# Folding the expert weights on TensorE, first rows in 13 pieces, and spare matrix products in an audio-tower kernel

## The reference, cut to what matters

```python
h = tok(x)                          # per feature: softplus/log gates and a log-space scan over 257 rows
h = h + attn(layernorm(h))          # 8 heads, 16 wide; sequence b attends to sequence b +- 4
h = h + ffn(layernorm(h))           # 16 experts, top 2, and one shared expert, all swiglu5
def ffn(x):
    h  = x @ w1 + b1                            # 128 -> 2*96 per expert
    g  = clip(h[..., ::2], -c0, c0); u = clip(h[..., 1::2], -c1, c1)
    t  = g * sigmoid(g * alpha) * scale * (u + shift)
    y += weight[expert] * (t @ w2 + b2)
```

## Time and profile before

| | |
|---|---|
| median of 3 runs | 325.62 us (325.33 to 325.69) |
| the profiled execution's own time | 325.96 us |
| its span, first to last instruction | 324.1 us |
| mean granted TensorE clock | 0.896 |
| busy: PE, DVE, ACT, POOL | 275.7, 255.6, 186.6, 128.8 us |

### The profile page before, as it was taken

The page is one execution under the profiler, slowest core; times in us unless marked ns, Lnnn a source line. Parts: engine busy times, 40 slices in busy tenths (PEclk is TensorE's granted clock), DMA queues, the critical chain, the costliest instruction groups (busy, mean ns, idle before and its releaser), DMA issues.

```text
span 324.1 us, 5121 instructions
## 1 busy us (share of the span) xinstructions
PE 275.7 (85%) x1764; PEld 169.3 (52%) x1764; DVE 255.6 (79%) x421; ACT 186.6 (58%) x297; POOL 128.8 (40%) x92
## 2 busy tenths in 40 slices
PE   3903941738998899999999999999999999999994
PEld 1301321305553666664466665566676699856641
DVE  1096878797559998779978879799578997599972
ACT  2757398653786878746487885186394620441151
POOL 2031959580204245582004437030735900654700
PEclk9965895575899999999999999999999975899798
DMA  6920000000000000000000000010010000000002
GB/s 235 418 91 0 0 2 0 2 0 0 2 2 1 1 2 3 0 2 0 0 3 2 0 1 2 2 33 2 0 34 0 2 0 0 3 1 0 2 1 65
DMA packets 3515, 7.41 MB, mean 23 GB/s; under 512 B 281, under 2 KB 2465, under 8 KB 3234
## 3 DMA queue, kind: packets, MB, share of 16 engines
q1 hardware_dynamic: 3490, 7.08, 5.9%
HBM read 6.03 MB, written 1.05 MB: 22 GB/s over the span
## 4 chain that ended last, share of the span: by engine, by line
PE 75%; issue 9%; DVE 9%; ACT 3%; DMA 1%; POOL 1%; DVEq 0%; SPq 0%; ACTq 0%
PE bank L1152 73%; DVE mxt L911 2%; PE bank L1155 2%; DVE w1l L805 2%; DMA cst<-in_consts 1%; DVE yr L976 1%; POOL z L461 1%; DVE tr L1008 1%; POOL z L466 1%; DVE vr L986 0%; ACT l L593 0%; DVE tr L1028 0%; DVE lt L832 0%; ACT osb L732 0%; DVE w L1046 0%
## 5 line engine op out<-in xcount | busy, mean ns | idle before, releaser
L527 POOL TENSOR_TENSOR vr<-vr,cwb 128x1024 f32<-128x1024 f32 x24 | 58.7, 2453 | 14.8 <-DVE vr L986 10.2
L1152 PE MATMUL bank<-tr,w 128*128 128x512 f32 (+1 forms) x104 | 50.0, 616 | 0.0
L911 DVE TENSOR_REDUCE mxt<-bank 128x2 f32<-128x512 f32 x64 | 40.5, 684 | 11.4 <-PE bank L1152 11.4
L1152 PE MATMUL bank<-xh,w1h 128*128 128x512 f32 x104 | 47.2, 454 | 0.8 <-DVE vr L986 0.8
L675 ACT ACTIVATE pt<-bank 128x512 f32<-128x512 f32 x64 | 33.8, 604 | 24.1 <-PE bank L1152 24.1
L726 ACT ACTIVATE tr<-yr,fpar 128x1024 f32<-128x1024 f32 (+1 forms) x28 | 30.0, 1086 | 27.0 <-PE bank L1152 17.0
L976 DVE TENSOR_SCALAR yr<-bank,fpar 128x512 f32<-128x512 f32 x52 | 40.2, 804 | 5.9 <-PE bank L1152 5.7
L521 POOL TENSOR_SCALAR vr<-vr,fpar 128x1024 f32<-128x1024 f32 x12 | 16.0, 1334 | 68.4 <-ACT vr L714 68.4
L1152 PE MATMUL bank<-xh,w1l 128*128 128x512 f32 x104 | 41.6, 400 | 0.0
L1152 PE MATMUL bank<-xl,w1h 128*128 128x512 f32 x104 | 41.4, 398 | 0.0
L1008 DVE SCALAR_TENSOR_TENSOR tr<-tr,yr 128x1024 f32<-128x1024 f32 (+1 forms) x28 | 33.5, 1213 | 2.8 <-ACT tr L726 2.7
(11 more groups left out here) (182 smaller groups left out, 480.8 us busy)
## 6 DMA issues: line engine op xcount, KB each, us to landing
pt<-in_w1a SPq DMA_DIRECT2D x1, 1672.0 KB, 9.3
tr<-in_w1b SPq DMA_DIRECT2D x1, 1672.0 KB, 12.4
xt<-in_x SPq DMA_DIRECT2D x4, 256.0 KB, 9.2
out<-osb SPq DMA_DIRECT2D x8, 128.0 KB, 1.9
w<-in_w SPq DMA_DIRECT2D x1, 832.0 KB, 14.1
cst<-in_consts SPq DMA_DIRECT2D x1, 488.5 KB, 5.0
cst<-in_consts SPq DMA_DIRECT2D x1, 193.5 KB, 4.3
vr<-in_shift SPq DMA_DIRECT2D x1, 6.5 KB
```

The lines of the kernel that those rows point to most:

```text
L527: g.tensor_tensor(vr[:, n % NV, :, :], vr[:, n % NV, :, :], cwb[:, u % 2, :].unsqueeze(1).to_broadcast([P, 2, W]), ALU.mult).then_inc(S["v ...
L911: last = v.tensor_reduce(top_of, ps.bank("mx", u, s, c, t)[:, :].rearrange("p (i t) -> p i t", i=2), AX_X, ALU.max)
L1152: return nc.tensor.matmul(out_, lhsT, rhs, start=start, stop=stop, **k)
```

## The change

- **Weights folded by TensorE.** `w1_row` is now 2 rows (the true row 0, and the shifts), where it was 128 (1672.0 KB). The transfer of `shift`, the pieces `w1s`, `w1p` and `gw` go. A new piece `wp` makes 7 parts of 512 columns (the last 256 and the 16 gate columns): identity by `w1_raw`, plus a 2-row product with a new constant `bsel`, both fp32, into one bank. `w1h` and `w1l` read the bank instead of `w1_raw`, and `w1l` releases it. A `g` or `u` product waits only for the parts that hold its columns; the first `pt` and `th` of unit 0 wait until the parts have been folded.
- **First rows in 13 pieces.** `zg` is 13 pieces of 4 products: the high weights by the high and low activations side by side (16 columns), and the low weights by the high ones (8 columns). `zclip` gets two more VectorE operations and clips out of SBUF. All pieces of the first rows move ahead of unit 3's experts, most of them into unit 2's attention.
- **Spare products.** 28 pieces `spare`, each of two fp32 products with 256 columns whose result nobody reads. Each waits for a milestone, a count of a semaphore of units 0 and 1 (`SPARE`), and takes and frees a bank.
- **All tables are new**: order on every engine and banks.

The new order of TensorE's pieces, up to the experts of unit 0: z.0.2 z.0.0 z.0.1 z.1.0 lsum.0 lsum.1 z.1.2 z.1.1 spare0 wp0 z.2.2 z.2.1 spare2 spare1 spare3 z.2.0 spare5 center.0.1 wp1 wp3 var.0.1 wp2 spare8 k.0 lsum.2 wp4 z.3.1 spare24 q.0 spare21 v.0 wp5 spare22 wp6 spare7 spare9 mx.0.0.0 mx.0.0.1 spare23 z.3.2 spare25 z.3.0 center.1.1 spare26 spare6 mx.0.1.0 nmt.0.0 spare10 var.1.1 spare4 lsum.3 mx.0.1.1 spare12 o0.0.0 spare27 st.0.0.0 nmt.0.1 q.1 k.1 st.0.0.1 pv.0.0.0 st.0.1.0 pv.0.0.1 st.0.1.1 o0.0.1 v.1 spare16 pv.0.1.0 mx.1.0.0 pv.0.1.1 mx.1.0.1 spare13 mx.1.1.0 center.0.2 spare17 center.2.1 mx.1.1.1 var.2.1 var.0.2 nmt.1.0 spare18 spare14 st.1.0.0 st.1.0.1 gate.0. Behind that, spare20 and spare19 stand in unit 0's experts, and spare15 and spare11 between the last `down` pieces of unit 3. The new `zg` order: zg.0 zgate zg.1 to zg.5, st.2.1.0, zg.6 to zg.9, st.2.1.1, down.1.4, zg.10 to zg.12, zcw, o0.2.1, pv.2.1.0, pv.2.1.1, mx.3.0.0, zd.

VectorE's new order: t.0 d.0 hg.0 l.0 w.0 mscan.0 dw.0 lf.0 w1l.0 sscan.0 w2s h1.0 w1l.1 xn.0.1 l.1 w1l.2 w.1 xsum.0 mscan.1 w1l.3 dw.1 l.2 w1l.4 w1l.5 w1l.6, and then the maxima of unit 0 with sscan.1, w.2, mscan.2, dw.2 and sscan.2 between them.

```diff
+SPARE = (("l3", 1), ("ll", 1), ("m", 2), ("dw", 1), ("s", 2), ("ef", 1), ("h1", 1), ("sq1", 1), ("rs1", 1), ("xs", 1), ("mz", 1),
+         ("mz", 2), ("nm", 2), ("nm", 4), ("lden", 1), ("lden", 2), ("h2", 1), ("h2", 2), ("sq2", 1), ("rs2", 1), ("xh", 1),
+         ("l3", 2), ("ll", 2), ("m", 4), ("dw", 2), ("s", 4), ("h1", 2), ("rs1", 2))
...
-            def w1p(u, k):
-                pool.wait_ge(s_w1s, 1)
-                pool.wait_ge(s_w1b, 16)
-                g.tensor_tensor(w1_raw[:, w1_part(k)], w1_raw[:, w1_part(k)], w1_row[:, w1_part(k)], ALU.subtract).then_inc(s_w1p, 1)
...
             def w1l_(u, k):
                 dve.wait_ge(s_w1h, k + 1)
-                v.tensor_tensor(w1l[:, w1_part(k)], w1_raw[:, w1_part(k)], w1h[:, w1_part(k)].bitcast(F32), ALU.subtract)\
-                    .then_inc(s_w1l, 1)
+                last = v.tensor_tensor(w1l[:, w1_part(k)], ps.bank("wp", 0, k)[:, 0:n], w1h[:, w1_part(k)].bitcast(F32), ALU.subtract)
+                ps.release(last, "wp", 0, k)
...
+            def wp(u, k):
+                pe.wait_ge(s_const, 16)
+                pe.wait_ge(s_w1a, 16)
+                pe.wait_ge(s_w1b, 16)
+                ps.take(pe, "wp", 0, k)
+                cols = slice(k * W, min((k + 1) * W, W1COLS + E))
+                o = ps.bank("wp", 0, k)[:, 0:cols.stop - cols.start]
+                mm(o, ident, w1_raw[:, cols], stop=False)
+                ps.fill(mm(o, const("bsel")[0:2, :], w1_row[:, cols], start=False), "wp", 0, k)
+
+            def spare(u, i):
+                ge(pe, *SPARE[i])
+                ps.take(pe, "spare", 0, i)
+                o = ps.bank("spare", 0, i)
+                ps.fill(mm(o[:, 0:T], wtok[:, 0:P], xt[:, 0, 0:T]), "spare", 0, i)
+                ps.release(mm(o[:, T:W], wtok[:, 0:P], xt[:, 0, T:W]), "spare", 0, i)
...
-                        mm(o, w1h[:, cols], zxh[:, :], stop=False)
-                        mm(o, w1h[:, cols], zxl[:, :], start=False, stop=False)
-                        last = mm(o, w1l[:, cols], zxh[:, :], start=False)
...
+                    mm(o, w1h[:, cols], zxs[:, :, :].rearrange("p k b -> p (k b)"), stop=False, skip_group_check=True)
+                    last = mm(o[:, 0:B], w1l[:, cols], zxs[:, 0, :], start=False, skip_group_check=True)
```

More of the change, by code:

```diff
@@ L34 @@
 for _name, _n in (("wtok", 3 * P), ("btok", 3), ("omat", P), ("cmat", P), ("wq", P), ("wk", P), ("wv", P), ("ident", P),
-                  ("head", 2), ("row", 2), ("nrow", 2), ("ones32", 64), ("e0sel", P), ("b2s", 1), ("par", 10)):
+                  ("head", 2), ("row", 2), ("nrow", 2), ("ones32", 64), ("e0sel", P), ("bsel", P), ("b2s", 1), ("par", 10)):
     CONSTS[_name] = (_at, _at + _n)
@@ L79, in unit_pieces @@
     f += [("yo", u), ("out", u), ("store", u)]
+    if u == 0:
+        a += [("spare", 0, i) for i in range(len(SPARE))]
     z = []
     if u == UNITS - 1:
-        z += [(n, 0) for n in ("zv", "zc", "zvar", "zrs", "zxn", "zone", "zsplit", "zgate", "zr1", "zexp", "zr2", "zcw", "zg",
-                               "zclip", "zth", "zgg", "zte", "zd", "zy", "zout", "zstore")]
+        z += [(n, 0) for n in ("zv", "zc", "zvar", "zrs", "zxn", "zone", "zsplit", "zgate", "zr1", "zexp", "zr2", "zcw")]
+        z += [("zg", 0, c) for c in range(NC)]
+        z += [(n, 0) for n in ("zclip", "zth", "zgg", "zte", "zd", "zy", "zout", "zstore")]
     return t + a + f + z
-SETUP_PIECES = [("w1s", 0)] + [(n, 0, k) for k in range(W1_PARTS) for n in ("w1p", "w1h", "w1l")] + [("gw", 0), ("w2s", 0)]
+SETUP_PIECES = [(n, 0, k) for k in range(W1_PARTS) for n in ("wp", "w1h", "w1l")] + [("w2s", 0)]
 PIECES = SETUP_PIECES + [p for u in range(UNITS) for p in unit_pieces(u)]
@@ L201, in filled_by @@
         return [("y0", u)]
-    one_bank = ("z", "lsum", "center", "var", "q", "k", "v", "nmt", "o0", "gate", "cwb", "g", "u", "out",
-                "zv", "zc", "zvar", "zgate", "zcw", "zg", "zd", "zout")
+    if name == "zg":
+        return [("zg", 0)] if numbers[0] == 0 else []
+    one_bank = ("wp", "spare", "z", "lsum", "center", "var", "q", "k", "v", "nmt", "o0", "gate", "cwb", "g", "u", "out",
+                "zv", "zc", "zvar", "zgate", "zcw", "zd", "zout")
     return [piece] if name in one_bank else []
@@ L339, in build @@
         s_zout = sem("first_rows_stored")
-        s_soft, s_w2s, s_w1s = sem("clamps"), sem("w2_scaled"), sem("w1_shifted")
-        s_w1p, s_w1h, s_w1l, s_gw = sem("w1_rows_taken"), sem("w1_high"), sem("w1_low"), sem("gate_weights")
+        s_soft, s_w2s = sem("clamps"), sem("w2_scaled")
+        s_w1h, s_gw = sem("w1_high"), sem("gate_weights")
         names = ("rh e3 l3 lp t d hg rl el ll w m dw ed s lf ef h1 sq1 sq2 rs1 rs2 xs one xh xl mz nm pv lden rd h2 "
-                 "rt rexp cwr gcv gcg ucv ucg th gg vcg vcv teg tev down zsq zrs zone zsplit zrt zexp zcwr zth zgg zte").split()
+                 "rt rexp cwr gcv gcg ucv ucg th gg vcg vcv teg tev down zsq zrs zone zsplit zg zsum zclip zrt zexp zcwr zth zgg zte").split()
         S = {n: sem("r_" + n) for n in names}
@@ L549, in zone @@
                 g.memset(zt[0:1, 4, :], 1.0).then_inc(S["zone"], 1)
-            run("G", {"w1p": w1p, "t": t_, "d": d_, "hg": hg, "dw": dw, "lf": lf, "h1": h1_, "h2": h2, "one": one_, "xl": xl_,
+            run("G", {"t": t_, "d": d_, "hg": hg, "dw": dw, "lf": lf, "h1": h1_, "h2": h2, "one": one_, "xl": xl_,
                       "gc": gate_clip, "uc": up_clip, "vc": weigh, "te": te, "zone": zone})
@@ L671, in pt_ @@
                 if u == 0 and s == 0:
-                    act.wait_ge(s_w1l, W1_PARTS)
-                    act.wait_ge(s_gw, 1)
+                    for k in range(W1_PARTS):
+                        ps.filled(act, "wp", 0, k)
                 ge(act, "pv", n - NPT + 1)
@@ L721, in th @@
                 if u == 0:
-                    act.wait_ge(s_gw, 1)
+                    for j in range(W1_PARTS):
+                        ps.filled(act, "wp", 0, j)
                 clipped(act, "g", GATE_BY, n, "gcv", "gcg")
@@ L767, in zth @@
                 act.wait_ge(s_par, PARS)
-                ps.released(act, "zg", 0)
+                ge(act, "zclip", 4)
                 for r, of in enumerate((slice(0, ROUTED), slice(ROUTED, NC))):
@@ L1090, in zclip @@
                 dve.wait_ge(s_par, PARS)
-                z = ps.bank("zg", 0)[:, 0:2 * NC * B].rearrange("p (k c b) -> p k c b", k=2, b=B)
+                z = ps.bank("zg", 0)[:, 0:4 * NC * B].rearrange("p (k c r b) -> p k c r b", k=2, c=NC, b=B)
+                v.tensor_copy(zsp, z[:, :, :, 1, :]).then_inc(S["zsum"], 1)
+                ge(dve, "zsum", 1)
+                last = v.tensor_tensor(zy[:, 0:2, :, :], z[:, :, :, 0, :], zsp, ALU.add)
+                ps.release(last, "zg", 0)
+                ps.released(dve, "zg", 0)
                 for kind, hi, lo in ((0, GHI, GLO), (1, UHI, ULO)):
                     for r, of in enumerate((slice(0, ROUTED), slice(ROUTED, NC))):
-                        last = v.tensor_scalar(zy[:, kind, of, :], z[:, kind, of, :], fpar[:, hi, r:r + 1], fpar[:, lo, r:r + 1],
-                                               ALU.min, ALU.max)
-                ps.release(last, "zg", 0)
+                        v.tensor_scalar(zy[:, kind, of, :], zy[:, kind, of, :], fpar[:, hi, r:r + 1], fpar[:, lo, r:r + 1],
+                                        ALU.min, ALU.max).then_inc(S["zclip"], 1)
             def zgg(u):
@@ L1141, in _ @@
             dve.wait_ge(s_bias, BIASES)
-            run("V", {"w1s": w1s, "w1l": w1l_, "gw": gw, "t": t_, "d": d_, "hg": hg, "l": l_, "w": w_, "mscan": mscan, "dw": dw,
+            run("V", {"w1l": w1l_, "t": t_, "d": d_, "hg": hg, "l": l_, "w": w_, "mscan": mscan, "dw": dw,
                       "sscan": sscan, "lf": lf, "h1": h1_, "h2": h2, "xn": xn, "xsum": xsum, "mr": mr, "mz": mz,
@@ L1271, in half_ @@
                 ge(pe, "xl", u + 1)
-                pe.wait_ge(s_w1l, W1_PARTS)
+                for k in sorted({(2 * c + kind) * P // W, ((2 * c + kind + 1) * P - 1) // W}):
+                    ps.released(pe, "wp", 0, k)
                 ps.take(pe, name, u, c)
@@ L1331, in zcw, with zg @@
                 ps.fill(mm(ps.bank("zcw", 0)[:, 0:B], zcwr[0:B, :, :].rearrange("p r e -> p (r e)"), ident[0:B, 0:B]), "zcw", 0)
-            def zg(u):
+            def zg(u, c):
                 ge(pe, "zsplit", 2)
-                pe.wait_ge(s_w1l, W1_PARTS)
-                ps.take(pe, "zg", 0)
+                for k in range(W1_PARTS):
+                    ps.released(pe, "wp", 0, k)
+                if c == 0:
+                    ps.take(pe, "zg", 0)
                 for kind in range(2):
-                    for c in range(NC):
-                        at = (kind * NC + c) * B
-                        o = ps.bank("zg", 0)[:, at:at + B]
-                        cols = slice((2 * c + kind) * P, (2 * c + kind + 1) * P)
-                        mm(o, w1h[:, cols], zxh[:, :], stop=False)
```

(12 more changed lines are left out.)

57 lines of the change are left out of this document (26 added, 31 removed), and 99 rows, old and new, of tables (AT, BANK_OF, BY).

## The result

The changed kernel takes 321.03 us in the median of 4 runs (320.70 to 321.59), the kernel before 325.48 on the same chip (325.26 to 325.69). The ratio is 0.9865, 95% interval 0.9847 to 0.9883: faster by 4.5 us, where the forecast was 14 (to 311.6 us, range 304 to 319). The span of the profiled execution is 318.9 us, before 324.1.

What follows compares the result with a forecast made beforehand. The head was taken as led by VectorE, the tail as TensorE's product work. First st of unit 1 at 98.7, plus 206.0 of tail and 5.4, gave a span of 310.1 and 311.6 us, range 304 to 319.

Steps and rivals of the forecast that it cites:

- The head: From unit 0's scans to unit 1's first st: that st starts at 98.7 us instead of 108.6, 9.9 earlier.
- The tail: From unit 1's first st to the last yo: product work on TensorE, 206.0 us instead of 210.1.
- neither bounds the tail (VectorE 129 of 151 us): Tail: fewer ScalarE table loads and two more VectorE operations in zclip cost nothing; without that cover some 0.5 us.
- minus 2.9: Tail, zg on TensorE: 52 products for 78, 26 fewer at 0.112 us each, saves 2.9 us.
- minus 5.0: Tail, clock around zg and zd: of 8.0 us lost before, 3.0 stay lost, so 5.0 us come back.
- The trace shows the clock low behind long gaps only: Head, TensorE's clock: reason for taking the high clock throughout, with the spares leaving no gap much over 2 us.
- The spares in the tail: Four spares on TensorE behind unit 1's first st: 3.4 us of work, of which 2.6 was kept as cost.
- the tail's spares fall into gaps: Rival, tail: the spares cost nothing (minus 2.6) and the clock holds through zg and zd (minus 3.0): 306.0 us; chance 0.2.
- No change: Rival, tail: fewer idle gaps but the same end, as VectorE takes over: 325.6 us; chance 0.03.
- seven `w1l` at 1.65 for 0.69: Head, VectorE: w1l parts from a bank take 0.69 us each; at 1.65 the seven would cost 6 us more.

Runs made afterwards that it cites:

- gps_load: Changed kernel with eight unused GpSimd operations of the old size put back at the places of w1p: 326.86 us, ratio 1.0046 to the kernel before.
- spares_out: Changed kernel without any of the 28 spare pairs: 324.31 us, ratio 0.996 to the kernel before.
- before_zg_short: Kernel before with 2 of the 13 blocks in zg, 12 thin products instead of 78: 320.81 us, ratio 0.9869 to the kernel before.
- te3_eighth: Changed kernel with VectorE's te of unit 3 on one column in eight: 318.01 us, ratio 0.9776 to the kernel before.
- before_te3: Kernel before with VectorE's te of unit 3 on one column in eight: 325.35 us, ratio 1.0005 to the kernel before.
- zg_short: Changed kernel with 2 of the 13 zg pieces, 8 thin products instead of 52: 318.44 us, ratio 0.9798 to the kernel before.

## Why the prediction was right and where it failed

- **The head** was right step by step: `center` 26.34 (forecast 27.7), `xn` 33.93 (34.4), `mx` 49.70 (49.8), the end of `nm.0.1` 71.45 (71.9), `st.1.0.0` 98.42 (98.7), `w1l` 0.69. One reservation: in the profiled execution the first `t` starts at 14.42 us, before at 15.71. No step forecast this. In the fourteen traces of the changed kernel and its variants the start varies from 14.26 to 15.66, in the three of the kernel before from 15.57 to 15.81, so part of the 1.3 us is luck, and whether the smaller `w1_row` has a part in it is not shown. From that start the head takes 84.0 us for 92.9, so the change itself is worth 8.9 of the 9.9 forecast. In gps_load and spares_out, one trace each, the head takes 4.9 and 2.6 us more on the same count (88.9 and 86.6); how the 8.9 divide is not shown beyond that.
- **The tail** failed: 215.1 us for 206.0. The terms on TensorE: idle 5.1 us more than before, where the forecast had none more; clock regained 1.7 (8.5 less 6.8), where it had 5.0; spares, as work, 3.4 for 2.6. That is 9.2 for the 9.1 missing.
- The step that failed is the sum of the tail: every microsecond of product work or low clock taken out of TensorE was put down as a microsecond of time, since "neither bounds the tail (VectorE 129 of 151 us)". That row ends at 260 us. From 257 to 308 us VectorE stood 4.9 us behind TensorE (before_zg_short and the waits shown there), and by the forecast's own figures the change takes 15 us out of TensorE at this place (`zg`, 78 by 0.112, and 6.4 of low clock). The last stage became VectorE's: te3_eighth takes 3.0 us out of the changed kernel and before_te3 none out of the one before. So the minus 2.9 and minus 5.0 had no full worth.
- The second term that failed is the clock's minus 5.0, which took `zg` in pieces for one dip of half the length. There are two dips, 5.1 and 1.7 us, and 1.7 came back. At its new place 4.9 us of products with 1.7 of clock are worth 2.2 to 2.6 us of time (zg_short), since TensorE then waits there. The forecast saw the pace of `zg` rightly (0.112 us from 192.50 to 195.30, 16 columns as 8) and asked whether small runs hold the clock. They do not; but without eleven of the thirteen pieces the clock falls as well, and what would hold it there stays open. "The trace shows the clock low behind long gaps only" was a wrong reading already then: in the earlier trace rows the pace halves in the middle of `zg` with TensorE busy all the time.
- **The spares in the tail** cost nothing, where 2.6 was put down: the rival "the tail's spares fall into gaps" had that right. The rival *No change*, by which VectorE takes over the tail, had the right mechanism for the last stage, and too low a chance.
- One slip in the working changed nothing: seven `w1l` at 1.65 for 0.69 cost 6.7 us more, not 6; they measured 0.68.

So the 9.9 forecast for the head came as 8.9, 1.3 came with the start, and the tail gave back 5.0: 5.2 of span, 4.5 in the medians.
